# Two layers of cross attention and experts on one core: the end of the first attention interleaved with the norm and the routing, and the token table split in two

## The reference, cut to what matters

```
x = x + L0_xattn(layernorm(x), ctx, ctx)      # 32 query heads, 8 key/value heads, head dim 16
x = x + L0_ffn(layernorm(x))                  # 16 experts, top 4, and a shared expert
x = x + L1_xattn(layernorm(x), ctx)           # 32 heads, 4 key/value heads, head dim 128
x = x + L1_ffn(layernorm(x))                  # gate with 8 experts, LoRA, top 2

L0_ffn: scores = sigmoid(x @ gate_w.T) + bias
        topk_w, topk_idx = top_k(scores, 4);  topk_w /= sum(topk_w)
        out[t] = sum over the 4 chosen e of topk_w * (silu(x Wg[e].T) * (x Wu[e].T)) @ Wd[e].T
        out   += silu(x Sg.T) * (x Su.T) @ Sd.T          # shared expert, every token
```

## Time and profile before

| what | us |
|---|---|
| median of 3 runs (lowest, highest) | 1271.15 (1268.21, 1271.93) |
| time of the profiled execution | 1268.94 |
| its span, first to last instruction | 1267.5 |
| TensorE busy in the span | 1205.7 |
| VectorE, ScalarE, GpSimd busy | 819.0, 682.0, 387.3 |
| mean granted TensorE clock, share of full speed | 0.991 |

### The profile page before, as it was taken

How to read it: one execution, slowest core, us unless ns; L and a number is a source line. 1 busy time by engine, 2 the same in 40 slices (tenths; PEclk the granted TensorE clock), 3 DMA queues, 4 the chain that set the end, 5 groups by cost and what they waited for, 6 DMA issues and landing times.

```text
span 1267.5 us, 16304 instructions
## 1 busy us (share of the span) xinstructions
PE 1205.7 (95%) x5820; PEld 930.8 (73%) x5820; DVE 819.0 (65%) x1529; ACT 682.0 (54%) x1561; POOL 387.3 (31%) x446
## 2 busy tenths in 40 slices
PE   8699987999999999899999999998999999999997
PEld 5556545767667677688888888877888888888765
DVE  4457765777776776665566666774455666667757
ACT  2245563167777787344555555662445555556621
POOL 3400010457777775002232322230022323222200
PEclk9899998999999999999999999999999999999999
DMA  8645240297579856521121221120311212211101
GB/s 292 149 122 140 52 180 38 100 336 171 103 155 242 254 116 129 183 83 41 44 67 59 67 59 42 59 83 25 92 38 47 67 59 64 62 42 51 58 1 66
DMA packets 73327, 127.91 MB, mean 101 GB/s; under 512 B 12120, under 2 KB 31448, under 8 KB 70552
## 3 DMA queue, kind: packets, MB, share of 16 engines
q1 hardware_dynamic: 54592, 76.00, 19.6%
q0 software_dynamic: 17296, 48.26, 15.1%
q10 hardware_dynamic: 1360, 2.62, 0.5%
HBM read 150.37 MB, written 26.48 MB: 140 GB/s over the span
## 4 chain that ended last, share of the span: by engine, by line
PE 68%; DVE 10%; issue 7%; POOL 7%; DMA 4%; ACT 3%; SPq 1%; ACTq 0%; POOLq 0%; DVEq 0%
PE bank L458 52%; PE bank L1935 7%; PE bank L1911 4%; POOL moe L1510 4%; POOL xs L1499 2%; PE bank L667 2%; DVE rden L853 1%; POOL wf_raw L1489 1%; DMA wf_raw<-in_wffn,weight_row 1%; PE bank L639 1%; PE bank L654 1%; PE bank L434 1%; DMA q0st<-m0T 1%; DMA q_rows<-q0T_lo 1%; DVE stats L395 1%
## 5 line engine op out<-in xcount | busy, mean ns | idle before, releaser
L1903 POOL TENSOR_SCALAR p<-p,mx 128x256 f32<-128x256 f32 x256 | 163.2, 653 | 521.8 <-DVE mx L1897 521.8
L1095 DVE TENSOR_TENSOR wf_lo<-wf_raw,wf_hi 128x512 fp32r<-128x512 f32 x192 | 124.4, 689 | 33.9 <-ACT wf_hi L1089 29.3
L1889 ACT ACTIVATE p<-bank,mx 128x256 f32<-128x256 f32 x256 | 118.0, 485 | 10.7 <-DVE mx L1879 10.6
L458 PE MATMUL bank<-xnA_hi,w1q_hi 128*128 128x512 f32 x288 | 118.5, 411 | 3.6 <-DVE xnA_lo L452 3.2
L1089 ACT ACTIVATE wf_hi<-wf_raw 128x512 fp32r<-128x512 f32 x192 | 110.2, 626 | 8.5 <-DMA wf_raw<-in_wffn,weight_row 8.1
L458 PE MATMUL bank<-xnA_hi,w1q_lo 128*128 128x512 f32 x288 | 114.6, 398 | 0.0
L458 PE MATMUL bank<-xnA_lo,w1q_hi 128*128 128x512 f32 x288 | 114.0, 396 | 0.0
L1918 ACT ACTIVATE p1T_hi<-bank 128x512 fp32r<-128x512 f32 x128 | 75.2, 596 | 65.7 <-PE bank L1911 65.7
L1843 ACT ACTIVATE q1T_hi<-bank 128x512 fp32r<-128x512 f32 x64 | 38.2, 597 | 132.5 <-PE bank L458 132.4
L458 PE MATMUL bank<-w1o_hi,a1T_hi 128*128 128x512 f32 x256 | 105.2, 411 | 0.1
L458 PE MATMUL bank<-wf_raw,zT 128*128 128x512 f32 x220 | 102.9, 593 | 2.2 <-DVE x L1169 1.3
(11 more groups left out here) (327 smaller groups left out, 3006.6 us busy)
## 6 DMA issues: line engine op xcount, KB each, us to landing
w_raw<-in_wq SPq DMA_DIRECT2D x64, 256.0 KB
w_raw<-in_wo SPq DMA_DIRECT2D x64, 256.0 KB
moe<-xn SPq DMA_DIRECT2D x2, 2304.0 KB, 10.4
returned<-moe SPq DMA_DIRECT2D x8, 512.0 KB, 7.7
q0st<-q_rows SPq DMA_DIRECT2D x14, 256.0 KB, 4.2
x<-in_x SPq DMA_DIRECT2D x8, 256.0 KB, 5.6
ctx<-in_ctxT SPq DMA_DIRECT2D x2, 1024.0 KB, 10.1
k0bd<-k_rows SPq DMA_DIRECT2D x16, 128.0 KB, 2.4
```

The source lines that it names most:

```text
L458: ins = nc.tensor.matmul(ps, a, b, start=(n == 0), stop=(n == len(pairs) - 1))
L1095: nc.vector.tensor_tensor(wf[m % 2][1][:, a, c, :], raw[m % STREAMS][:, a, c, :], wf[m % 2][0][:, a, c, :].bitcast(F32), ALU.subtract).the ...
L1889: ins = nc.scalar.activation(pr1[s % 2][:, h, :], banks.of(("s1", s, n))[:, hh * 2 * P:(hh + 1) * 2 * P], ACT.Exp, bias=m[:, UH + h:UH + h ...
L1903: ins = nc.gpsimd.tensor_scalar(pr1[s % 2][:, h, :], pr1[s % 2][:, h, :], m[:, 3 * UH + h:3 * UH + h + 1], 1.0, ALU.mult, ALU.mult)
```

## The change

**End of the attention.** The loops end at i = 63. `before_experts` and the bank ring `yrs` go. Side work gets places of its own: weight splits at i = 38, 40, 42, 44 as before; the gate's weights at 46; `norm(2, j)` at 39, 43, 45, 47, 49, 51, 53; the gate product of batches 0 to 3 at 54, its transpose at 58; the choice for these batches on VectorE at 59, and a first half of the ranks (`tensor_ranks_first`, 4 matmuls) at 61. VectorE takes the statistics of batches 4 to 7 (`norm_stats(3, ...)`) behind each projection's add. Behind the loop TensorE has y0(6), gu(0), y0(7); ScalarE has the last sums, a one-column square root on a constant, and the last split; VectorE has `vector_slots_first` (7 instructions), then the last batch's reciprocals.

**Shared expert.** Banks are named by hand instead of by rings. gu(n) runs further ahead of dn(n). `tensor_ranks` has 9 matmuls in place of 16, `vector_slots` one more. `row_hot` is two tables of half the size, the first made before the second gate. The token table becomes two products of 32 matmuls: `tensor_tokens` (48 columns) behind dn(4), and `tensor_token_shares` (96 columns) behind the transposes of z(6) and z(7). `tile_share` goes from GpSimd to VectorE, behind the token numbers; `vector_weight_rows` goes behind the second `row_hot`. ScalarE's split for tile 1 now waits for the shares product. `tensor_x_turn(0)` goes ahead of dn(7).

**GpSimd.** Seven small iotas move ahead of the wait for the last scores. The order before the tiles becomes gather(0), weights(1), gather(1), weights(2), gather(2), gather(3), weights(3), weights(4).

```diff
         LEAD_S, LEAD_T = 14, 2
-        EXPERTS_FROM = UNITS0 // 2 + 4
         LAG_Y = 9
+        SPLIT_AT = {38: 0, 40: 1, 42: 2, 44: 3}
+        NORM2_AT = {39: 0, 43: 1, 45: 2, 47: 3, 49: 4, 51: 5, 53: 6}
+        GATE_SPLIT, GATE_AT, GATE_TURN_AT, CHOICE_AT, RANKS_AT = 46, 54, 58, 59, 61
...
-            for i in range(-LEAD_S, UNITS0 + LAG_Y + 1):
+            for i in range(-LEAD_S, UNITS0):
...
+                if NORM2_AT.get(i, 0) >= 3:
+                    norm_turn(2, NORM2_AT[i] - 3, 7 if i < UNITS0 - LEAD_S else next(srs))
+                if i == GATE_AT:
+                    tensor_gate(0, 0)
...
-            tensor_gate_turn(0, next(yrs))
+                if i == GATE_TURN_AT:
+                    tensor_gate_turn(0, 1)
+                if i == RANKS_AT:
+                    tensor_ranks_first(0)
+            project_out(B - 2, 7)
+            tensor_gate_up(0, 6)
+            project_out(B - 1, 3)
...
+            sums_out(B - 1, 1)
+            nc.scalar.activation(first_col[:, 0:1], eps, ACT.Sqrt)
+            attended(B - 1)
...
+                    if b >= HB:
+                        dve.wait_ge(S["y0_add"], b + 1)
+                        norm_stats(3, b - HB)
...
+                if i == CHOICE_AT:
+                    vector_gate(0)
+                    vector_choice(0)
+            vector_slots_first()
...
+        def tensor_tokens(n):
+
+            ps = banks.take(n, "tokens", (S["token_in"], 2))
+            pe.wait_ge(S["tile_hot"], 2)
+            for i in range(PAIRS):
+                h, at = divmod(i, PAIRS // 2)
+                pe.wait_ge(S["row_hot"], h + 1)
+                ins = nc.tensor.matmul(ps[:, 0:TILE_COLS], row_hot[h][:, at, :], tile_hot[:, i, 0, :],
+                                       start=(i == 0), stop=(i == PAIRS - 1))
...
+            tensor_down(4, 4)
+            tensor_tokens(5)
+            tensor_down(5, 6)
+            tensor_gate_up(7, 2)
+            tensor_z_turn(6, 7)
+            tensor_z_turn(7, 3)
+            tensor_token_shares(5)
+            tensor_down(6, 7)
+            tensor_x_turn(0)
+            tensor_down(7, 3)
...
+            act.wait_ge(S["tokens"], 2)
             for c in range(4):
                 scalar_gu(1, c)
...
             gather(0)
+            pool.wait_ge(S["weight_row"], 1)
+            weights(1)
             gather(1)
+            weights(2)
             pool.wait_ge(S["zero_fill"], 32)
+            pool.wait_ge(S["token_in"], 2)
+            gather(2)
+            gather(3)
             pool.wait_ge(S["routed"], 1)
             weights(3)
-            gather(2)
-            gather(3)
```

More of the change, by code:

```diff
@@ L1221, in vector_choice, with tensor_ranks_first @@
             nc.vector.tensor_copy(taken[:, bs, :], slot_of_e[:, bs, :]).then_inc(S["taken"], 1)
-        def tensor_ranks():
-            ps = banks.take(next(turn_ring), "ranks", (S["at_row"], 1))
+        def tensor_ranks_first(n):
+            ps = banks.take(n, "ranks0", (S["row_hot"], 1))
+            pe.wait_ge(S["taken"], 1)
+            pe.wait_ge(S["rank_consts"], 3)
+            flat = taken[:, :, :].rearrange("p b e -> p (b e)")
+            nc.tensor.matmul(ps[:, 0:HB * E0], below[:, :], flat[:, 0:HB * E0], start=True, stop=False)
+            for d in range(1, HB):
+                ins = nc.tensor.matmul(ps[:, d * E0:HB * E0], ones_r[:, :], flat[:, 0:(HB - d) * E0], start=False,
+                                       stop=(d == HB - 1))
+            ins.then_inc(S["ranks"], 1)
@@ L1226, in tensor_ranks @@
+        def tensor_ranks(n):
+            ps = banks.take(n, "ranks", (S["at_row"], 1))
             pe.wait_ge(S["taken"], 2)
-            pe.wait_ge(S["rank_consts"], RANK_CONSTS)
             flat = taken[:, :, :].rearrange("p b e -> p (b e)")
-            nc.tensor.matmul(ps[:, 0:B * E0], below[:, :], flat, start=True, stop=False)
-            for d in range(1, B):
-                nc.tensor.matmul(ps[:, d * E0:B * E0], ones_r[:, :], flat[:, 0:(B - d) * E0], start=False,
-                                 stop=(d == B - 1))
@@ L1233, in tensor_ranks @@
-            for b in range(B):
-                ins = nc.tensor.matmul(ps[:, B * E0:(B + 1) * E0], ones_r[:, :], taken[:, b, :], start=(b == 0),
-                                       stop=(b == B - 1))
-            ins.then_inc(S["ranks"], 1)
+            for d in range(1, B + 1):
+                first = max(HB, d)
+                nc.tensor.matmul(ps[:, (first - HB) * E0:(HB + 1) * E0], ones_r[:, :],
+                                 flat[:, (first - d) * E0:(B + 1 - d) * E0], start=(d == 1), stop=False)
@@ L1335, in vector_tokens @@
         def vector_tokens():
-            ps = banks.of("tokens")
-            up, part = ps[:, 0:TILES], [ps[:, c * TILE_COLS:c * TILE_COLS + TILES] for c in (1, 2)]
+            up = banks.of("tokens")[:, 0:TILES]
             dve.wait_ge(S["tokens"], 1)
@@ L1379, in scalar_shared @@
             scalar_silu(1)
+            scalar_silu(2)
             scalar_gate(1)
```

268 lines of the change are left out of this document (146 added, 122 removed).

## The result

The changed kernel takes 1275.13 us (median of 6 runs, 1274.30 to 1278.39), the kernel before beside it 1271.34 (6 runs): ratio 1.0039, 95% interval 1.0022 to 1.0055. It is slower by a little more than the 0.3% that the prediction took for no change, though the interval does not exclude less. The profiled execution took 1275.03 us (span 1273.6), the one before 1268.94 (span 1267.5).

A forecast was written before the change was run, and what follows sets the result against it. TensorE was taken as the bound, over two thirds of the chain, the rest waits. Tiles −1.9 and clock +1.3 gave −0.6 us: 1268.3 against the profiled 1268.94, 1270.5 as median; range 1263.5 to 1276.5.

The forecast's parts named there:

- The gain at the scaling: End of the attention: scaling of norm batches 4 to 7 from 207.5 instead of 210.10 us, −2.6.
- the clock: New TensorE waits at unit 46 and first ranks: fall behind the second costs 2.6 us, counted half, +1.3; first mostly hidden.
- Unit 43: Attention's end: the norm's root between exponentials delays that of unit 46, +3.6 us; y0(4) at 164.0 instead of 158.20, +5.8.
- Units 50 to 61: Attention's end: unit 54 at 176.3, gate product to 180.4, choice done at 194.3, TensorE standing 3.3 us before the first ranks.
- Rival 3: Attention's end: clock falls behind both waits, +2.9 us each, 1275.1; decides if unit 63 ends behind 199; chance 0.25.
- Token product −9.65: Shared expert: product ends at 242.7 instead of 252.3 us, gather(0) issued at 244.1 instead of 253.73, −9.65.
- The price by the number of matmuls: Token products: cost goes by the number of matmuls, not columns; the second product costs +3.6 us.
- From there to gu(8): Token product's end, 242.7 us, to the first tile's product, 257.5 instead of 262.21; shared expert's sum −4.7.
- The tiles, +2.8: Expert tiles: weights of tiles 1 and 2 take 9.0 us of crowded DMA; the lead shrinks from −4.7 to −1.9 us.

The follow-up runs named there:

- run 3: Changed kernel with the norm's steps at units 48 to 55 and gate, choice and first ranks two units later; 1271.95 us, 1.0004 of the kernel before.
- run 11: Changed kernel with only the norm's steps moved late, to units 48 to 53; 1274.07 us, 1.0008 of the kernel before.
- run 9: Changed kernel with 30 extra, unread transposes filling TensorE's first long wait, at unit 46; 1275.62 us, 1.0025 of the kernel before.
- run 10: Changed kernel with 26 extra, unread transposes filling TensorE's second long wait, ahead of the first ranks; 1274.05 us, 1.0008 of the kernel before.
- run 4: Changed kernel with the first token product at 96 columns instead of 48, the added ones unread; 1275.84 us, 1.0034 of the kernel before.
- run 8: Changed kernel with norm, gate, choice and ranks later, weights of tiles 1 and 2 ahead of the gathers, one 144-column token product; 1268.02 us, 0.9970.
- run 1: Changed kernel with the weight loads of tiles 1 and 2 ahead of the gathers; 1274.57 us, 1.0021 of the kernel before.
- run 2: Changed kernel with extra, unread transposes filling both long waits of TensorE, 30 at unit 46 and 26 ahead of the first ranks; 1274.28 us, 1.0021.
- run 7: Changed kernel with norm, gate, choice and ranks later and the weights of tiles 1 and 2 ahead of the gathers; 1269.32 us, 0.9984.
- run 12: Kernel before with one edit: weights of tiles 1 and 2 behind the first and second gather; 1279.03 us, 1.0052 of the kernel before.
- run 5: Changed kernel with weights of tiles 1 and 2 ahead of the gathers and one 144-column token product instead of two; 1273.30 us, 1.0017.

## Why the prediction was wrong

The sum was −0.6 us, the profile after has +4.2 (and 1.5 of the opening). Two steps failed. The gain at the scaling of batches 4 to 7, put at −2.6, was +1.8 and +2.4: units 50 to 61 take 2.0 longer than said, and the last reciprocals come late. And the clock, put at 1.3 for half of one fall, cost 1.5 to 2.1 at that fall and came down once more before the first tile, where nothing was counted. By the prediction's own steps, with the 1.5 us of the opening taken off every position:

- **Unit 43: right.** Said: exponential of 46 through at 156.8, y0(4) at 164.0. Measured 156.9 and 164.3. The stall is the prediction's 3.6 (3.68). Runs 3 and 11 show that it is the place of the norm's steps: with them at unit 48 and later y0(4) is back where it was.
- **Units 50 to 61: 2.0 too short.** Said: unit 54 at 176.3, gate through at 180.4, choice done at 194.3. Measured 177.1, 182.2 and 196.3. Part of it is a wait of 0.99 for the norm's low part ahead of the gate product, which was given no time. The wait for the choice itself was sized right (3.3 said, 2.99 measured).
- **The clock: counted half, and at one place of two.** Both waits brought a fall. That the first lies under other waits was right (run 9: 0.2 us at y0(4)). The second was put at 2.6 and halved to 1.3; run 10 measures 1.5 to 2.1 at y0(7). The nearest row had said that the clock falls, and I gave the density of the work ahead of the wait as a reason for half. No row supported it. This alone is 0.2 to 0.8 too little; the larger part is the fall ahead of the first tile, below. In all, TensorE is at 0.50 for 17.1 us between 150 and 290 in both executions of the changed kernel, and for 6.8 before. The medians point the same way. Of the 31 executions of the kernel before beside the second profile, the two with a mean clock of 0.985 took 1272.94 and 1274.98 us, the twelve with 0.991 took 1269.09 to 1272.36; the changed kernel's eight had 0.984 or 0.985 and took 1274.59 to 1277.58. By these rows I estimate that some 3 of the 5 us go with the lower clock. No run holds the clock fixed, so this is not shown as a cause.
- **The gain at the scaling, −2.6: not there.** Measured +1.8 and +2.4. Of the miss of 4.4, the choice has 2.0; unit 63 ends at 199.8 instead of 196.7, 1.1 more, with the attention products at half clock; and the last reciprocals, sums and splits, from the end of unit 63 to y0(7), take 6.7 instead of 5.8; 0.4 fall behind y0(7). Rival 3 had its point of decision at 199. It was passed by 0.8, and it decided as written: the last reciprocals came late.
- **Token product −9.65: right in itself.** From the scaling to the end of the product are 35.4 us, 35.2 in the prediction's numbers. All of the filling of the shared expert up to there was sized right: ranks, banks, the order of the products. The price by the number of matmuls holds: 48 columns 4.05 us, 96 columns 4.07 in the same place (run 4), 144 columns 3.77 (run 8). "TensorE: Matmul & The Clock Gate", Back-to-back issue gap, of the Trainium skill has the isolated matmul at its columns over 2.4 GHz and 2.5 ns, by which I estimate 0.7 us for 32 of 48 columns; the same section says that this counts too little where every matmul has a weight load of its own, and gives 81 ns for 128 columns there. The prediction quoted the first of the two. The rows, 0.127 a matmul, lie above both.
- **From there to gu(8): 2.6 too short.** Said 14.8, measured 17.4. Two terms were missing in this execution: half clock from 249.4 to 252.8, some 1.7 us, and the first tile's own weights, 1.8 us too late, which shows as TensorE's wait of 1.94 instead of 1.07. Over all runs the length of this stage goes with the clock. Seven executions with two products (the second of the changed kernel, 1, 2, 3, 7, 9, 11) have 6.8 us at 0.50 in stage B and a B of +0.6 to +0.8, whether the loads stand first (1, 7) or not; the two with 10.2 us (4 and 10) have +2.5 and +1.9. In the second execution of the changed kernel the weights are only 0.4 late, in runs 9, 10 and 11 the splits wait for the product and not for them. So putting the loads first wins nothing that can be read in stage B; its gain is in the tiles. The prediction knew that the loads moved into the crowd, but never set the landing of tile 1's against its need. Run 12 prices that move alone, on the kernel before, at 0.52%; there the first tile does stand for them.
- **The tiles, +2.8: the size was right**, +1.6 and +3.1 in two executions. Run 1 shows the cause: with the loads first it is +0.2. The four runs with the loads first (1, 5, 7, 8) have −0.7 to +0.9, the eight executions of the changed kernel and its variants with them behind the gathers +0.8 to +3.3.

So the mechanism of rival 3, a long wait for the choice with the clock behind it, took part in the attention's loss, but not as it was priced. It had 2.9 and 2.9 for the two falls, and the first costs nothing that can be read. That its 1275.1 meets the measured 1275.13 is luck: terms of which it did not speak, the late choice and the half clock ahead of the first tile, made up for that. The miss of the point is 4.8 us, from −0.6 to +4.2: stage A 4.4 and stage B 2.9 too short, less 1.3 of reserve and 1.2 in the tiles.

Two things stay open. One is the fall of the clock between 244.7 and 265.6 us. It occurs at shifting places in all ten executions with two token products, with no wait over 1.1 us ahead of it since the scaling; filling waits or widening matmuls did not remove it. The kernel before has none there, and runs 5 and 8, with one product, have theirs only at the waits of 3.73 and 3.78 us for the gathered rows. So it goes with the split of the token table, and the cost of the split is more than the 3.6 of the second product; why is not shown. The other is that run 10's time is better than its stages say (1.0 us over before by the ratio, 3.4 by the stages of its one profile). Its profiled execution is the slowest of its twelve (1275.52, median 1274.05), and the profile before lies 2.4 below its median, which is the size and direction of the gap.

## What to carry to other kernels

Before a small serial step (root, choice) is moved into a full loop, look which long operations stand ahead of it on the engine that feeds it, and place it behind the loop's own hand-over, not between its exponentials: the same norm held y0(4) back by 6.1 us at unit 43 and by nothing at 48. A load whose address is known early belongs in the quiet stretch; putting it behind a transfer on the critical path moves it into the crowd, and the first to wait is the consumer with the least slack, in run 12 the first tile, with all that is queued behind its splits. A gain in TensorE's idle time is no gain in time where the clock falls with it: compare the time at 0.50 of both kernels as well. Where a wait in the nearest row brought a fall of the clock, count the whole fall behind a wait of the same length.

## What the runs showed of the hardware

- Every wait of TensorE from 2.88 to 4.84 us between 150 and 275 us had a granted clock of 0.50 at it, begun in the wait or within 0.8 us of its end: 2.88 and 4.84 (run 12), 2.89 (before), 2.99, 3.00 and 3.68 (the changed kernel and its variants), 3.73 and 3.78 (runs 5 and 8). One of 3.67 in run 12 lies in the fall behind its 4.84. Eight waits of 2.06 or 2.07 had none. Below lies no clean line: one of 2.45 had a fall in run 3 and none in runs 7, 8 and 11, and in run 7 the clock fell at 197.3, 1.8 us behind a wait of 1.80 that had none in runs 3 and 8. In runs 2, 9 and 10 transposes that nobody reads, 0.11 us each, put in the place of the wait, kept it at 1.00.
- The length of such a fall differs for the same code: 6.8 us in the profile of the kernel before (199.6 to 206.4), 3.4 in run 12 (200.9 to 204.3), whose program is the same up to there. y0(7) starts 148.9 behind the transfer in both, and stage A is 1.1 shorter in run 12.
- An indirect load of 1.57 MB issued among gathers landed 9.2 us after its issue, one in run 12 after 9.8. "Trainium Kernel Development and Optimization", Key Constraints, of the Trainium skill says that all queues share 16 engines and interleave; no run separates the queues, and the 0.99 busy at 369 GB/s shows only that the engines were full. Issued ahead of the gathers (242.76 in run 1), the same load was not waited for.
- With 32 matmuls in a row, 48, 96 and 144 columns cost 0.127, 0.117 to 0.127, and 0.115 to 0.118 us each at full clock.
